# Two-block metaformer on one core: gate product taken before the normalisation, last yv quad ahead of the first turning, choice split

## The reference, cut to what matters

```
x = x + L0_conv(ln_c(x))                 # 3x3 neighbourhood attention, 4 heads
t = tokens(x);  t = t + L0_ffn(ln_t(t))  # experts choose tokens
x = x + L1_conv(ln_c(x))                 # 9x9 patches, a @ (b^T @ c) / r
t = tokens(x);  t = t + L1_ffn(ln_t(t))  # a loop of steps, each chosen from token 0

# L0_ffn, 16 experts, 8 tokens for each
logits = x @ gate_w.T + gate_b
probs = softmax(logits, over the tokens)
topv, topi = top_k(probs, 8)
pooled[e] = sum over k of x[topi[k, e]] * topv[k, e]
h = gelu([pooled, 1] @ weight1[e]);  out = [h, 1] @ weight2[e]
outputs[topi[k, e]] += out * topv[k, e]
```

## Time and profile before

| | us |
|---|---|
| median of 3 runs (115.15 to 118.18) | 115.47 |
| profiled execution, its own time | 115.39 |
| its span | 113.4 |
| TensorE busy | 101.1 (89%) |
| vector engine busy | 60.9 (54%) |
| ACT busy | 43.0 (38%) |
| GpSimd busy | 65.3 (58%) |

### The profile page before, as it was taken

How to read it: one execution, slowest core, us unless ns; L and a number is a source line. 1 busy time by engine, 2 the same in 40 slices (tenths; PEclk the granted TensorE clock), 3 DMA queues, 4 the chain that set the end, 5 groups by cost and what they waited for, 6 DMA issues and landing times.

```text
span 113.4 us, 2244 instructions
## 1 busy us (share of the span) xinstructions
PE 101.1 (89%) x825; PEld 66.2 (58%) x825; DVE 60.9 (54%) x146; ACT 43.0 (38%) x96; POOL 65.3 (58%) x67
## 2 busy tenths in 40 slices
PE   5999979949889999998999999989999989987750
PEld 4756726729334357666868665643498866554440
DVE  0047299797599998005451420199517447035980
ACT  4271620334000004060487456623230453756742
POOL 8993299500757898999991000199999940009100
PEclk9999999999999999999999999999999999999999
DMA  3933700000000000000000000000000000100014
GB/s 88 300 41 70 132 6 0 0 0 6 0 0 0 3 0 0 6 0 0 0 0 3 0 6 0 0 3 0 0 6 0 0 0 0 29 6 3 0 52 162
DMA packets 7148, 2.61 MB, mean 23 GB/s; under 512 B 5454, under 2 KB 6624, under 8 KB 7137
## 3 DMA queue, kind: packets, MB, share of 16 engines
q1 hardware_dynamic: 6849, 2.04, 7.8%
q10 hardware_dynamic: 288, 0.43, 1.0%
HBM read 1.87 MB, written 0.59 MB: 22 GB/s over the span
## 4 chain that ended last, share of the span: by engine, by line
PE 62%; DVE 22%; ACT 6%; issue 4%; POOL 2%; DVEq 1%; ACTq 0%; POOLq 0%
PE PS L613 8%; DVE prods L1263 7%; PE PS L899 6%; PE PS L742 5%; PE PS L727 5%; PE PS L825 4%; DVE prods L1301 4%; PE PS L629 3%; PE PS L880 3%; PE PS L642 3%; PE PS L619 3%; PE PS L819 3%; PE PS L872 2%; PE PS L720 2%; PE PS L910 2%
## 5 line engine op out<-in xcount | busy, mean ns | idle before, releaser
L1065 ACT ACTIVATE sq<-PS 128x288 f32<-128x288 f32 x16 | 6.3, 418 | 25.2 <-PE PS L727 19.9
L613 PE MATMUL PS<-sq 128*128 128x288 f32 (+1 forms) x44 | 14.6, 452 | 1.1 <-POOL sq L493 1.1
L1301 DVE TENSOR_TENSOR prods<-PS,vpad 128x432 f32<-128x432 f32 x24 | 12.8, 600 | 1.9 <-PE PS L742 1.6
L533 POOL TENSOR_TENSOR prods<-prods 128x576 f32<-128x576 f32 x8 | 11.8, 1481 | 3.0 <-DVE prods L1301 2.8
L727 PE MATMUL PS<-prods,cst 128*128 128x288 f32 x44 | 12.4, 420 | 0.2 <-POOL prods L533 0.2
L572 POOL TENSOR_TENSOR x<-h,x 128x192 f32<-128x192 f32 x6 | 4.5, 782 | 13.3 <-ACT h L1146 13.3
L727 PEld LDWEIGHTS PS<-prods,cst 128*128 128x128 f32 x44 | 7.8, 189 | 5.5 <-POOL prods L533 1.9
L613 PEld LDWEIGHTS PS<-sq 128*128 128x128 f32 x44 | 8.2, 208 | 4.1 <-POOL sq L493 1.1
L561 POOL TENSOR_TENSOR x<-x,prods 128x576 f32<-128x576 f32 x7 | 9.8, 1406 | 0.5
L519 POOL TENSOR_TENSOR prods<-q_sb,kpad 128x576 f32<-128x576 f32 x6 | 7.7, 1334 | 4.1 <-ACT kpad L1094 4.1
L1263 DVE TENSOR_TENSOR prods<-PS,kpad 128x576 f32<-128x576 f32 x12 | 8.1, 749 | 2.3 <-ACT kpad L1094 2.3
(11 more groups left out here) (165 smaller groups left out, 189.7 us busy)
## 6 DMA issues: line engine op xcount, KB each, us to landing
result<-y SPq DMA_DIRECT2D x2, 288.0 KB, 2.8
prods<-in_x SPq DMA_DIRECT2D x2, 144.0 KB, 2.9
prods<-in_x ACTq DMA_DIRECT2D x1, 288.0 KB, 3.5
cst<-consts SPq DMA_DIRECT2D x1, 261.5 KB, 3.0
ew<-in_L_ffn_weight SPq DMA_DIRECT2D x4, 64.0 KB, 2.3
ew<-in_L_ffn_weight SPq DMA_DIRECT2D x1, 256.0 KB, 2.9
cst<-consts SPq DMA_DIRECT2D x1, 160.0 KB, 2.9
cst<-consts ACTq DMA_DIRECT2D x1, 128.0 KB, 2.9
```

The source lines that it names most:

```text
L533: return nc.gpsimd.tensor_tensor(tap(a), tap(a), tap(b), ALU.add).then_inc(padd_rdy, 1)
L613: nc.tensor.matmul(PS[:, bank, 0:width], sq[:, 0, 0:P], sq[:, 0, 0:width], start=True, stop=True)
L1065: nc.scalar.activation(sq[:, t, px], src, ACT.Square).then_inc(sq_rdy, 1)
L1301: nc.vector.tensor_tensor(prods[:, t, m * TRI:(m + 1) * TRI, q * QS:(q + 1) * QS].rearrange("p n (r c) -> p n r c", c=WW), PS[:, ring(2 * ...
```

## The change

It alters two stretches. In L0_ffn the gate product is taken from `xc` instead of `y`: half 0 before the variances, half 1 after them (before rstd is there). `rstd` is spread over the rows of the logits (one expert and image each) by four products with a new constant `rows_e`, ACT copies the raw gate product to `gated`, and the vector engine multiplies the two into `logit`. The vector engine, not ACT, copies the second half of `xc`. The gate bias no longer enters `logit`; it enters the exponent's bias in two small operations. `xc` instead of `y` is turned for `yT`, in other banks and with a wait for the first copy ahead of the fifth pair, and ACT copies it before the exponential. For the pooled values `pick` is multiplied by the spread `rstd` (`pick_n`). The `y` of this part is not formed. Filler products are removed behind the variances of i = 1 and behind its `widen`.

In L1_conv's end, yv 4 comes ahead of turning 0; the vector engine copies quad 3 with two copies ahead of `token`, ACT the other four; and the x3 sum of t = 0 is put inside `choose(0)`, behind the index and ahead of the register load, the one of t = 1 behind it.

```diff
@@ tensor
+            def gate(t):
+                pe.wait_ge(xc_copied, T + t + 1)
+                for g in range(2):
+                    last = nc.tensor.matmul(PS[:, GATE_BANK + g, 0:HS], gate_bd[:, t, :], cut(xc, t)[:, g, :],
+                                            start=(t == 0), stop=(t == T - 1), skip_group_check=True)
+                    if t == T - 1:
+                        last.then_inc(logit_done, 1)
+            gate(0)
             variances(1)
-            widen(1)
+            gate(1)
+            pe.wait_ge(rstd_rdy, 2)
+            for q in range(4):
+                last = nc.tensor.matmul(PS[:, VB[1] + q, 0:QS], by_expert(q), rstd[32 * q:32 * q + 32, :],
+                                        start=True, stop=True, skip_group_check=True)
+            last.then_inc(rwide_rdy, 1)
...
             for c in range(FULL + 1):
                 w = P if c < FULL else TAIL
+                if c == FULL:
+                    pe.wait_ge(yT_rdy, 1)
                 for t in range(T):
-                    last = nc.tensor.transpose(PS[0:w, 4 + c // 2, ((c % 2) * T + t) * P:((c % 2) * T + t + 1) * P],
-                                               y[:, t, c * P:c * P + w], idn)
+                    last = nc.tensor.transpose(PS[0:w, TURN_BANK[c // 2], ((c % 2) * T + t) * P:((c % 2) * T + t + 1) * P],
+                                               xc[:, t, c * P:c * P + w], idn)
...
-            pe.wait_ge(logit_rdy, 2)
+            pe.wait_ge(yT_rdy, 3)
+            keep_clock(2, 1)
             preload(0)
-            keep_clock(2, 7)
...
             yv_quad(2)
             yv_quad(3)
+            yv_quad(4)
             pe.wait_ge(yv_rdy, 3)
             turn_back(0)
-            yv_quad(4)
-            keep_clock(1, 5)
-            pe.wait_ge(yv_rdy, 5)
+            keep_clock(1, 3)
+            pe.wait_ge(yv_rdy, 4)
+            pe.wait_ge(yv3_rdy, 1)
             turn_back(1)
@@ scalar
             layernorm(1, eps5)
-            act.wait_ge(gb_ld, 16)
             for g in range(2):
                 act.wait_ge(logit_done, g + 1)
-                nc.scalar.activation(logit[:, g * HS:(g + 1) * HS], PS[:, g, 0:HS], ACT.Identity,
-                                     bias=gb[:, :]).then_inc(logit_rdy, 1)
+                nc.scalar.copy(gated[:, g * HS:(g + 1) * HS], PS[:, GATE_BANK + g, 0:HS]).then_inc(gate_copied, 1)
+            for c in range(0, FULL + 1, 2):
+                act.wait_ge(yT_done, c // 2 + 1)
...
             act.wait_ge(ntop_rdy, 1)
-            nc.scalar.activation(half(0, PROB_BANK), flat2(logit[:, :]), ACT.Exp, bias=ntop[:, :],
+            nc.scalar.activation(half(0, PROB_BANK), flat2(logit[:, :]), ACT.Exp, bias=shift[:, :],
...
-            for k in range(5):
+            for k in (0, 1, 2, 4):
                 yv_copy(k)
@@ vector
+                if i == 1:
+                    for g in range(2):
+                        dve.wait_ge(gate_copied, g + 1)
+                        nc.vector.tensor_tensor(two(logit[:, g * HS:(g + 1) * HS]), two(gated[:, g * HS:(g + 1) * HS]), wide_e(g),
+                                                ALU.mult).then_inc(logit_rdy, 1)
+                    return
...
-            layernorm(1, y)
+            for g in range(2):
+                dve.wait_ge(sq_rdy, 2 * (T + 1) + g + 1)
+                last = nc.vector.tensor_copy(cut(xc, 1)[:, g, :], PS[:, XB[1][1] + g, 0:HS])
+            last.then_inc(xc_copied, 1)
+            layernorm(1, None)
...
-            nc.vector.tensor_scalar(ntop[:, :], top8[:, 0:1], -1.0, None, ALU.mult).then_inc(ntop_rdy, 1)
+            dve.wait_ge(gb_ld, 16)
+            nc.vector.tensor_scalar(ntop[:, :], top8[:, 0:1], gb[:, :], -1.0, ALU.add, ALU.mult).then_inc(max_rdy, 1)
+            dve.wait_ge(max_rdy, 1)
+            nc.vector.tensor_tensor(shift[:, :], ntop[:, :], gb[:, :], ALU.add).then_inc(ntop_rdy, 1)
...
+                dve.wait_ge(pick_rdy, g + 1)
+                nc.vector.tensor_tensor(two(pick_n[:, cells]), two(pick[:, cells]), wide_e(g), ALU.mult).then_inc(pickn_rdy, 1)
...
             dve.sem_inc(fw_free, 1)
+            dve.wait_ge(yv_done, 4)
+            for r in range(2):
+                last = nc.vector.tensor_copy(by_group((QUADS[3][0] + r) * GRP, 2), PS[V2 * r:V2 * (r + 1), YV_BANK[3], 0:2 * GW]
+                                             .rearrange("k (g p j) -> k g p j", g=2, p=NPT))
+            last.then_inc(yv3_rdy, 1)
...
-            choose(0, token[:, 0:NOPS])
-            for t in range(T):
...
+            choose(0, token[:, 0:NOPS], after={2: lambda: x3_sum(0)})
+            x3_sum(1)
```

More of the change, by code:

```diff
@@ L39 @@
 _COLS = [("idn", P), ("cen", P), ("mean", T * 32), ("heads", T * P), ("hsum", T * 32), ("own", B), ("blk", GV), ("blk_end", GV_END),
-         ("ebias", P), ("istep", NB_)]
+         ("ebias", P), ("rows_e", P), ("istep", NB_)]
 OFF, _o = {}, 0
@@ L82, in constant_table @@
     put("ebias", (e[:, None] == p[None, :] // B).astype(np.float32))
+    img = (p % 32) // HEADS
+    put("rows_e", ((p[:, None] % HEADS == 0) & (img[:, None] == p[None, :] % B)).astype(np.float32))
     put("istep", 4 * NOPS * np.arange(NB_, dtype=np.float32)[None, :])
@@ L141, in metaformer @@
         share = sb("share", [P, P])
-        prob = sb("prob", [P, S])
+        pick_n = sb("pick_n", [P, S])
+        shift = sb("shift", [P, 1])
+        gated = sb("gated", [P, S])
         pick = sb("pick", [P, S])
@@ L249, in metaformer @@
                              "pool_steps"))
-        wc_rep = sem("wc_rep")
+        wc_rep, yv3_rdy = (sem(n) for n in ("wc_rep", "yv3_rdy"))
         tail_rdy, bc_ld, bc_set = (sem(n) for n in ("tail_rdy", "bc_ld", "bc_set"))
+        gate_copied, max_rdy, pickn_rdy = (sem(n) for n in ("gate_copied", "max_rdy", "pickn_rdy"))
         row2_done, row2_rdy, row3_rdy = (sem(n) for n in ("row2_done", "row2_rdy", "row3_rdy"))
@@ L286, in metaformer, with by_expert, wide_e, two @@
         XB, VB = ((0, 2), (2, 0), (0, 6), (0, 2)), (4, 4, 2, 4)
+        def by_expert(q):
+            return cst[32 * q:32 * q + 32, OFF["rows_e"][0]:OFF["rows_e"][1]]
+        def wide_e(g):
+            return PS[:, VB[1] + 2 * g:VB[1] + 2 * g + 2, 0:QS]
+        def two(a):
+            return a.rearrange("p (u s) -> p u s", u=2)
         def cut(a, t):
@@ L338, in metaformer @@
         MAB_BANK = [6, 7, 5, 0, 1]
-        PICK_BANK = (7, 2)
+        PICK_BANK = (4, 2)
+        GATE_BANK = 2
+        TURN_BANK = (0, 1, 0)
         PROB_BANK = 2
@@ L398, in by_patch, with by_group @@
             return a[:, 0:ALL * GW].rearrange("k (g p j) -> k p g j", g=ALL, p=NPT)[:, 2 * i:2 * i + pair(i), :, :]
+        def by_group(first, n):
+            a = yvT[:, first:first + GRP]
+            return bass.AP(a.tensor, a.offset, [a.ap[0], [2 * GRP, n], [B * C, NPT], [1, GRP]])
         def gw_of(g):
@@ L631, in variances @@
                 last.then_inc(var_rdy, 1)
-                if i != 2:
+                if i in (0, 3):
                     keep_clock(2, VB[i] + 1)
@@ L646, in widen @@
                 last.then_inc(rwide_rdy, 1)
-                if i < 2:
+                if i == 0:
                     pe.wait_ge(xc_copied, T * i + 1)
@@ L807, in _ @@
                 w = P if c < FULL else TAIL
-                pe.wait_ge(pick_rdy, 1 if c * P + w <= HS else 2)
-                last = nc.tensor.matmul(PS[0:w, PICK_BANK[c // FULL], (c % FULL) * P:(c % FULL + 1) * P], pick[:, c * P:c * P + w],
+                pe.wait_ge(pickn_rdy, 1 if c * P + w <= HS else 2)
+                last = nc.tensor.matmul(PS[0:w, PICK_BANK[c // FULL], (c % FULL) * P:(c % FULL + 1) * P], pick_n[:, c * P:c * P + w],
                                         share[:, :], start=True, stop=True, skip_group_check=True)
@@ L867, in pixels_out @@
                     pe.wait_ge(scat_copied, i + 1)
-                pe.wait_ge(y_rdy, 2 * T + T * (i + 1 if i < 2 else NP))
+                pe.wait_ge(y_rdy, T + T * (i + 1 if i < 2 else NP))
                 for t in range(T):
@@ L1076, in layernorm @@
                 nc.scalar.activation(rstd[:, :], vlog[:, :], ACT.Exp, scale=-0.5).then_inc(rstd_rdy, 1)
-                keep(1)
+                if i != 1:
+                    keep(1)
             def log_exp_table():
@@ L1110, in _ @@
             layernorm(1, eps5)
-            act.wait_ge(gb_ld, 16)
             for g in range(2):
                 act.wait_ge(logit_done, g + 1)
-                nc.scalar.activation(logit[:, g * HS:(g + 1) * HS], PS[:, g, 0:HS], ACT.Identity,
-                                     bias=gb[:, :]).then_inc(logit_rdy, 1)
+                nc.scalar.copy(gated[:, g * HS:(g + 1) * HS], PS[:, GATE_BANK + g, 0:HS]).then_inc(gate_copied, 1)
+            for c in range(0, FULL + 1, 2):
+                act.wait_ge(yT_done, c // 2 + 1)
+                n, w = (2, P) if c < FULL else (1, TAIL)
```

(9 more changed lines are left out.)

7 lines of the change are left out of this document (removed).

## The result

The changed kernel took 117.56 us (median of 4, 116.99 to 117.96) against 115.92 for the kernel before on the same occasion; the ratio is 1.0169, 95% interval 1.0121 to 1.0216. It is slower by 1.7%, where 0.9% faster was forecast, and outside the range. Ratios and their intervals leave out executions more than 1.5% above the fastest of the same kernel, while medians count them all. The profiled execution of the changed kernel took 117.96, with a span of 115.7 against 113.4.

The account below looks back on a forecast made before the run. The prediction took a chain of waits in two stretches, not TensorE's busy share, to bound the kernel. From 115.39 us, 1.6 gained in L0_ffn and 0.6 lost at L1_conv's end gave 114.4 us, range 113.3 to 115.5.

Parts of the forecast that it names:

- the transposes around 52 to 54: Ten transposes of xc in L0_ffn, with gaps, where a halved granted clock was thought possible.
- part B: L1_conv's end: last quad early, fourth quad by the vector engine, choice split; cost 0.6 us (0.3 to 0.9).
- Part A: L0_ffn: gate product taken before the normalisation and scaled afterwards; gain 1.6 us (0.9 to 2.0).
- variances: Variance products after gate(0) in L0_ffn; 0.65 us, bounds 0.6 and 0.94.
- by_expert: Four products instead of eight ahead of the gated copies in L0_ffn; 0.42 us, between 0.38 and 0.75.
- the multiplications: Two logit multiplications of 128x288 ahead of max8 in L0_ffn; 0.44 us each.
- Given back: Between max8 and prec in L0_ffn: a second 128x1 operation on ntop before exp; +0.21 us.
- ctrl: The choice's result at L1_conv's end, which SP's weight DMAs await; late by 0.95 to 1.4, taken as 1.2 us.
- h of the last normalisation: Output of LN3 after L1_conv; LN3 gains 0.1 us, bounds -0.15 and +0.4.
- The base: The profiled execution of the kernel before, 115.39 us, from which the sum started.
- Rival 1: At L1_conv's end, part B costs nothing as the token has room; 113.7 us, chance 0.22.
- rival 3: The clock falls in the gap around 52 to 54; +4.5, so 118.9 us, chance 0.06.

Follow-up runs that it names:

- e4: The changed kernel with three filler products instead of one ahead of the loop; 114.88 us, ratio 0.9899.
- e2: The kernel before with part B alone; 117.62 us, ratio 1.0143.
- e1: The changed kernel with part B undone and part A kept; 117.34 us, ratio 1.0129.
- e11: The changed kernel with only the load of fb2 issued earlier, second behind the first layer's bias; 116.07 us, ratio 0.9963.
- e7: The changed kernel with shift summed by tensor_scalar with a pointer operand, and three filler products instead of one ahead of the loop; 114.97 us, ratio 0.9910.

## Why the prediction was wrong

**The clock.** The prediction weighed a fall at 0.06, gave it the right sign and a price (+4.5 us) that was too high, and looked for it in the wrong place, at the transposes around 52 to 54. There it did not fall: TensorE's gaps were at most 0.45 us, and even the 1.12 us at 57 for which it waited for pick_n, late through shift, left the granted clock at 1.00. The step that failed is the clock's place in the sum: no term at all, on the ground that "No row of before shows a fall". That was true of one execution, and half of the kernel's executions have one. The working of part B had x3b holding `tok_h` in front of the token's product, with the products of the loop behind it, but counted this as time on the chain and not as idleness of TensorE. Against the pooling product the token's product came only 0.09 later; but h came 0.69 earlier, so TensorE was through with its first hidden products sooner and then idle for 0.54 us. In place of the missing term the profiles have +1.66 us from the token's product to the end, most of the loss, and e4 shows that it goes when the fall does.

**Part A.** To max8 the gain was 2.58 (forecast 2.42). The terms held: variances 0.63 (0.65), by_expert 0.50 (0.42), the multiplications 0.83. From prec to the pooling product +0.81 (forecast +0.61). The step that failed is "Given back: ntop now has a second operation before exp ... +0.21". It was priced by prec, which has one input, in SBUF, and ran in the same stretch of GpSimd sums without harm; the new operation has two. It measured 1.34, and max8 to prec rose by 1.44 instead of 0.21. With the pointer form the whole part gives 1.45 against 1.6. So the mechanism was right, and the one mis-sized term took 1.1 us of it.

**Part B.** Forecast cost 0.6, measured 0.09 in the profiles and 0.10 in e2. ctrl was 0.67 late on the common scale (95.20 against 93.98, with all of the stretch 0.55 later), not 1.2: the register load hides wholly under the x3 sum, and cand came at 94.97, just before the pair of sums was over (94.23 + 0.82 = 95.05). For the same reason x3_sum(1) came early, and h of the last normalisation was 0.69 earlier, not 0.1. The last load and x3b held the token as described: x3b ends and tok_h starts, with no wait. This mechanism was right, its price too high, and its consequence for TensorE's clock unseen. The fall does not need it, though: e1, without part B, fell in 4 of 4.

**The base.** 115.39 was a lucky execution for the sum: short first products and no fall at the end. The kernel before has a median of 116.6 over its 65 other executions, and against that the changed kernel's 117.56 is 1.0 us slower and not 1.6. By stretches the forecast was -1.6 for part A and +0.6 for part B, -1.0 in all; the profiles show -0.33 and +0.09, and beside them +0.88 at the start and +1.66 in the loop, for which the sum had nothing. Rival 1 (part B costs nothing) held for the chain, rival 3 (the clock) for the sign.

## What to carry to other kernels

An operation of one element for each partition costs as much as what it waits for: give a short vector operation beside long GpSimd operations one SBUF tensor and a pointer (0.21 us here) or a PSUM operand, not two SBUF tensors (1.34). Where TensorE waits on a chain of other engines late in a kernel, count its idle time as a risk to its clock and not only as the chain's delay, and look at several executions' granted clocks before trusting one profile. A change that saves work can be worth less than two filler products in the gap that it leaves.

## What the runs showed of the hardware

- A tensor_tensor of 128x1 with both inputs in SBUF took 1.33 to 1.35 us while GpSimd ran an addition of 128x576, and ended 0.01 to 0.02 us behind it (the changed kernel, e1, e4, e11). The same sum by tensor_scalar with a pointer took 0.21 beside the same addition.
- The first products vary in length by execution: eight passes of 288 columns from 4.18 took between 2.12 and 3.27 us. The granted clock reads 1.00 there in all profiles.
- A fall at the loop's entry cost 1.5 us between the medians of the kernel before (115.7 and 117.2). In e7 a fall that lasted only to about 108 (granted clock 0.67, 0.50 and 0.56 from 104 to 105, to 106 and to 108) cost about 0.9 between the medians of its executions with and without a fall: 115.2 against 114.3.
- The vector engine's queue executed a register load behind two additions while they still ran: cand came 0.74 us after the first of them started, with 0.82 for the pair, though the load alone is 0.33.
